# A third GpSimd addition for each group, another table of shared units and slots, and a prologue with two token chains side by side

## The reference

```python
# tokens: b=64, t=128, j=64
h = layernorm(x.reshape(b, t, 192), ln0_g, ln0_b)
h = relu(conv2d(h, conv1_w, conv1_b, ((2, 2), (1, 1))))     # 128 -> 128 channels, 5x3
h = relu(conv2d(layernorm(h), conv2_w, conv2_b, ...))       # 5x2
h = relu(conv2d(layernorm(h), conv3_w, conv3_b, ...))       # 128 -> 256 channels, 5x2
h = layernorm(concat(...)) @ out_w + out_b                  # [b, 128, 64]

# attention on xn = layernorm(h), 8 heads of width 64
v = xn @ wqv_w.T + wqv_b                                    # q, vf, vb
k = xn[:, :, None, :] * wk
a = -sum_w |q[b,s,h,w] - k[b,t,h,w]| / 8                    # L1 distance, no matmul form
a = softmax(concat(a, zeros(1 row)), axis=1)[:, :t]
o = (einsum('bsdh,bshw->bdhw', a, vf) + einsum('bdsh,bshw->bdhw', a, vb)).sum(heads)
h = h + xn + (o * sigmoid(1.702 * o)) @ fanin_w.T + fanin_b

# experts: 32 of width 16, the one with the greatest logit for each token
h = h + relu(relu(xn @ W1[idx] + b1[idx]) @ W2[idx] + b2[idx])   # xn = layernorm(h)
```

## Time and profile before

| | |
|---|---|
| median of three timed executions | 3646.7 us (3644.56 to 3649.15) |
| profiled execution | 3643.14 us, span 3641.3 us |
| mean granted TensorE clock | 0.973 |
| VectorE busy | 3320.0 us (91%), 2699.7 of them direct reductions (2272) |
| TensorE busy | 3261.5 us (90%) |
| ScalarE busy | 2621.0 us (72%), 1863.9 of them absolute values (1824) |
| GpSimd busy | 2435.1 us (67%) |
| accumulating DMAs | 512, 478.18 MB, 66.7% of 16 engines |

### The profile page before, as it was taken

The page is one execution under the profiler, slowest core; times in us unless marked ns, Lnnn a source line. Parts: engine busy times, 40 slices in busy tenths (PEclk is TensorE's granted clock), DMA queues, the critical chain, the costliest instruction groups (busy, mean ns, idle before and its releaser), DMA issues. The chain is left out here.

```text
span 3641.3 us, 77565 instructions
## 1 busy us (share of the span) xinstructions
PE 3261.5 (90%) x23008; PEld 2460.2 (68%) x23008; DVE 3320.0 (91%) x4557; ACT 2621.0 (72%) x4705; POOL 2435.1 (67%) x2212
## 2 busy tenths in 40 slices
PE   5899999999999999999999999999999999999886
PEld 4667667666677666677666677666677666677554
DVE  4899999999999999999999999999999999999885
ACT  1677777777777777777777777777777777777774
POOL 1676667676766766766766676766666766666764
PEclk8999999999999999999999999999999999999998
DMA  1677777777777777777777777777777777777774
GB/s 56 133 156 148 142 144 149 142 150 148 140 145 148 141 157 146 141 144 149 143 151 146 142 142 151 146 147 145 146 142 146 153 145 146 145 144 139 156 143 84
DMA packets 192483, 516.99 MB, mean 142 GB/s; under 512 B 67990, under 2 KB 126230, under 8 KB 151352
## 3 DMA queue, kind: packets, MB, share of 16 engines
q0 software_dynamic: 73728, 478.18, 66.7%
q1 hardware_dynamic: 118712, 38.26, 5.3%
HBM read 10.79 MB, written 2.10 MB: 4 GB/s over the span
## 5 line engine op out<-in xcount | busy, mean ns | idle before, releaser
L788 DVE TENSOR_REDUCE S<-psU 128x16 f32<-128x1024 f32 x2272 | 2699.7, 1215 | 190.2 <-PE psU L387 169.1
L387 PE MATMUL psU<-flat,kT 99*128 99x256 bf16 x16384 | 2304.7, 276 | 233.5 <-DVE S L788 205.2
L587 ACT ACTIVATE absd<-psU 128x1024 f32<-128x1024 f32 x1824 | 1863.9, 1024 | 612.3 <-PE psU L387 589.2
L387 PEld LDWEIGHTS psU<-flat,kT 99*128 99x128 bf16 x16384 | 1508.8, 98 | 871.1 <-DVE S L788 389.3
L1056 POOL TENSOR_TENSOR absd<-absd 128x1024 f32<-128x1024 f32 (+2 forms) x512 | 1111.3, 2171 | 307.5 <-DMA absd<-absd 304.4
L1045 POOL DMA_DIRECT2D absd<-absd x512 | 456.4, 891 | 640.5 <-ACT absd L587 571.0
L1060 POOL TENSOR_TENSOR absd<-absd 128x512 f32<-128x512 f32 (+2 forms) x512 | 586.0, 1145 | 40.1
L400 PE MATMUL psC<-c1in,w 128*128 128x256 f32 (+1 forms) x960 | 347.4, 449 | 21.3 <-DVE c1in L830 21.2
L799 DVE TENSOR_REDUCE S<-absd 128x64 f32<-128x512 f32 (+2 forms) x512 | 315.7, 617 | 7.6 <-POOL absd L1060 7.6
L486 PE MATMUL psZ<-P,v 128*128 128x256 f32 x1024 | 301.3, 387 | 0.8 <-ACT P L701 0.8
L419 PE MATMUL psC<-c3in,w 128*128 128x128 f32 x1280 | 256.2, 286 | 23.1 <-DVE c3in L830 23.1
(11 more groups left out here) (139 smaller groups left out, 2076.1 us busy)
## 6 DMA issues: line engine op xcount, KB each, us to landing
absd<-absd POOLq DMA_DIRECT2D x320, 1024.0 KB, 7.7
absd<-absd POOLq DMA_DIRECT2D x160, 768.0 KB, 6.4
flat<-qparts SPq DMA_DIRECT2D x3072, 8.0 KB, 3.7
absd<-absd POOLq DMA_DIRECT2D x32, 512.0 KB, 4.8
xin<-in_x SPq DMA_DIRECT2D x32, 192.0 KB, 7.0
out_h<-result SPq DMA_DIRECT2D x32, 64.0 KB, 5.7
w<-in_w SPq DMA_DIRECT2D x1, 1280.0 KB
w<-in_w SPq DMA_DIRECT2D x1, 960.0 KB, 5.2
```

The source lines that it names most:

```text
L387: mm = nc.tensor.matmul(psU[:, slot % PLACES, m], kT[0:ROWS + 3, b, m, :], flat[0:ROWS + 3, half % HALVES, :, lo:lo + BLOCK], start=True, ...
L587: nc.scalar.activation(absd[:, c % GROUPS, :, u], psU[:, slot % PLACES].rearrange("p (n a) s w -> p n (a s w)", n=2), ACT.Abs).then_inc(a_ ...
L788: nc.vector.tensor_reduce(S[:, b, hd, SB * c:SB * c + SB], psU[:, slot % PLACES].rearrange("p a s w -> p s a w"), AX.XY, ALU.add, apply_ab ...
```

## The change

1. GpSimd's tree gets a third level. After 16 + 16 and 8 + 8, it now adds 4 + 4, so VectorE's last addition reduces four numbers for each sum and not eight (WIDTH = 4, LEVELS = 3). The tree stands 11 slots behind the group's end and not 10; the last addition stays at 17.
2. 60 of the 128 units are shared and not 57: groups of four, three and two units number 13, 2 and 1, where they numbered 10, 5 and 1.
3. Nearly all slots of the tables move by a few.
4. The prologue has one loop of 256 slots. The chain of pair 0 runs in psL, the second bank of psU's last place, with semaphores of its own (lead_pe and so on), and the chain of pair 1 in psC, 40 slots behind (LEAD). As both share the input tiles c1in, c2in, c3in, resn and resT, the second waits for the first chain's reader in each (`lead(step)`). Norm and keys of pair 0 start at slot 128, the first queries at 128 + QUERY_AFTER = 194 plus their own slots.
5. VectorE's twelve copies into `flat` go. SyncE issues four DMAs with 96 partitions each, as soon as the pattern is there, behind the load of the third pair's input.

```diff
-SHARED = [(0, 2, 4, 6), (0, 2, 4, 6), (1, 3, 5), (0, 2, 4, 6), (0, 2, 4, 6), (0, 2, 4, 6), (1, 3, 5), (0, 2, 4, 6),
-          (0, 2, 4, 6), (0, 2, 4, 6), (0, 4), (2, 4, 6), (0, 2, 4, 6), (0, 2, 4, 6), (0, 3, 6), (0, 2, 4)]
+SHARED = [(0, 2, 4, 6), (0, 2, 4, 6), (0, 2, 4, 6), (0, 2, 4, 6), (1, 3, 5), (0, 2, 4, 6), (0, 2, 4, 6), (0, 2, 4, 6),
+          (0, 2, 4, 6), (0, 2, 4, 6), (0, 2, 4, 6), (3, 6), (0, 2, 4, 6), (0, 2, 4, 6), (0, 3, 6), (0, 2, 4, 6)]
...
-LEVELS = 2
-WIDTH = 32 >> LEVELS
-TREE_AFTER = 10
+LEVELS = 3
+WIDTH = 4
+TREE_AFTER = 11
+LEAD = 40
+QUERY_AFTER = 66
...
-KQ_AT = dict(kT=21, q=13, q_len=1, qpart1=12, qrest1=13, qpart2=28, qpart3=29)
+KQ_AT = dict(kT=21, q=13, q_len=1, qpart1=13, qrest1=14, qpart2=38, qpart3=37)
...
+        psL = psU[:, PLACES - 1, BLOCKS // 2:BLOCKS].rearrange("p m s w -> p (m s w)")
...
             def prologue():
                 load_x(1)
                 load_x(2)
+                sp.wait_ge(pattern_made, 14)
+                for n in range(HALVES):
+                    heads = slice(n % 2 * 4, n % 2 * 4 + 4)
+                    sp.dma_start(flat[0:ROWS, n],
+                                 pattern[0:ROWS, heads].rearrange("p h m w -> p (h m w)").unsqueeze(1)
+                                 .broadcast_to([ROWS, SB, HALF])).then_inc(filled, 16)
...
                 pe.wait_ge(ready, READY)
-                for s in range(SLOTS):
+                for s in range(2 * SLOTS):
                     if s == TOK_AT["conv2"]:
                         pe.wait_ge(loaded, LOADED)
-                    tok(0, s)
-                for s in range(SLOTS):
-                    norm(0, s)
-                    kq(0, 0, s - SECOND)
-                    tok(1, s)
+                    tok(0, s, psL, lead_pe, lead_act, lead_dve)
+                    norm(0, s - SLOTS)
+                    kq(0, 0, s - SLOTS - QUERY_AFTER)
+                    tok(1, s - LEAD)
...
+                def lead(step):
+
+                    if isinstance(p, int) and p == 1:
+                        dve.wait_ge(lead_pe, TOK_PE.after(0, step))
...
                 nc.gpsimd.tensor_tensor(lo, lo, hi, ALU.add).then_inc(a_tree, 1)
+                rows = lo.rearrange("p u (s w) -> p u s w", w=BLOCK)
                 pool.wait_ge(a_tree, LEVELS * (TREES * i + c) + 1)
-                rows = lo.rearrange("p u (s w) -> p u s w", w=BLOCK)
+                lo, hi = rows[:, :, :, 0:8], rows[:, :, :, 8:16]
+                nc.gpsimd.tensor_tensor(lo, lo, hi, ALU.add).then_inc(a_tree, 1)
+                pool.wait_ge(a_tree, LEVELS * (TREES * i + c) + 2)
                 lo, hi = rows[:, :, :, 0:WIDTH], rows[:, :, :, WIDTH:2 * WIDTH]
                 nc.gpsimd.tensor_tensor(lo, lo, hi, ALU.add).then_inc(a_tree, 1)
```

More of the change, by code:

```diff
@@ L362, in unit @@
                 if slot == 0 and isinstance(i, int) and i == 0:
-                    pe.wait_ge(filled, 3 * HALVES)
+                    pe.wait_ge(filled, 16 * HALVES)
+                if slot == PLACES - 1 and isinstance(i, int) and i == 0:
+                    pe.wait_ge(lead_dve, TOK_DVE.after(0, "h"))
                 if slot % 64 == 0:
@@ L395, in tok @@
                     if n == 0:
[L396 to L399 removed]
+                        pe.wait_ge(by_dve, TOK_DVE.after(q, "shifta1"))
+                    o_v = z[:, 0:6 * J].rearrange("p (b j w) -> p b j w", b=2, w=3)
                     mm = nc.tensor.matmul(o_v[:, :, :, o:o + wn], w1[:, 3 * dy + dx, :],
@@ L610, in tok @@
                 if slot == TOK_AT["turn"] + 1:
-                    act.wait_ge(tok_pe, TOK_PE.after(p, "turn"))
-                    nc.scalar.activation(resT[:, :, :], psC[:, 0:2 * T].rearrange("p (b t) -> p b t", b=2),
+                    act.wait_ge(by_pe, TOK_PE.after(q, "turn"))
+                    if isinstance(p, int) and p == 1:
+                        act.wait_ge(lead_pe, TOK_PE.after(0, "out"))
+                    nc.scalar.activation(resT[:, :, :], z[:, 0:2 * T].rearrange("p (b t) -> p b t", b=2),
@@ L835, in after, with tok @@
+            def tok(p, slot, z=psC, by_pe=tok_pe, by_act=tok_act, by_dve=tok_dve, by_pool=tok_pool):
+                q = max(p - 1, 0) if isinstance(p, int) else p - 1
+                def lead(step):
+                    if isinstance(p, int) and p == 1:
+                        dve.wait_ge(lead_pe, TOK_PE.after(0, step))
                 def after(name):
-                    return lambda s: TOK_DVE.after(p, s[:-1] + name + s[-1])
+                    return lambda s: TOK_DVE.after(q, s[:-1] + name + s[-1])
@@ L860, in tok @@
+                    lead("turn")
                     for b in range(2):
                         nc.vector.tensor_scalar(resn[:, b, :], rows(2 * J)[:, b, :], mv["d"][:, b, 0:1],
-                                                rstd["d"][:, b:b + 1], ALU.subtract, ALU.mult).then_inc(tok_dve, 1)
+                                                rstd["d"][:, b:b + 1], ALU.subtract, ALU.mult).then_inc(by_dve, 1)
                 if slot == TOK_AT["out"] + 1:
-                    dve.wait_ge(tok_pe, TOK_PE.after(p, "out"))
+                    dve.wait_ge(by_pe, TOK_PE.after(q, "out"))
@@ L870, in norm @@
             def norm(p, slot):
                 if slot == NORM_AT["stat"]:
-                    dve.wait_ge(tok_dve, TOK_DVE.after(p, "h"))
+                    if isinstance(p, int) and p == 0:
+                        dve.wait_ge(lead_dve, TOK_DVE.after(0, "h"))
+                    else:
+                        dve.wait_ge(tok_dve, TOK_DVE.after(p - 1, "h"))
                     stats(h, "n", norm_dve, lambda s: NORM_DVE.after(p, s))
@@ L998, in prologue @@
                         weigh()
-                        fill(0)
-                    if s == TOK_AT["conv3"]:
-                        fill(1)
-                for s in range(SLOTS):
-                    norm(0, s)
-                    kq(0, 0, s - SECOND)
-                    tok(1, s)
-                    if s == TOK_AT["conv1"]:
-                        fill(2)
+                    norm(0, s - SLOTS)
+                    kq(0, 0, s - SLOTS - QUERY_AFTER)
+                    tok(1, s - LEAD)
             def iteration(i, late=True, tokens=True, ahead=True):
@@ L1124, in prologue @@
                 pool.wait_ge(ready, READY)
-                for s in range(SLOTS):
-                    if s == TOK_AT["conv2"]:
-                        pool.wait_ge(loaded, LOADED)
-                    tok(0, s)
-                for s in range(SLOTS):
-                    norm(0, s)
-                    kq(0, 0, s - SECOND)
-                    tok(1, s)
+                for s in range(2 * SLOTS):
+                    tok(0, s, lead_dve, lead_pool)
+                    norm(0, s - SLOTS)
+                    kq(0, 0, s - SLOTS - QUERY_AFTER)
+                    tok(1, s - LEAD)
             def iteration(i, late=True, tokens=True, ahead=True):
```

155 lines of the change are left out of this document (77 added, 78 removed).

## The result

The changed kernel takes 3586.24 us, the median of three runs (3582.9 to 3590.83), against 3646.7: a ratio of 0.9838, 95% interval 0.9824 to 0.9851. It is faster, by 60 us. I had forecast 3490 us, and 3580 was the upper end of my range: the forecast gain was 157 us, and less than half of it came.

The account below looks back on a forecast made before the run. The bound was taken to alternate in each pair, about 63 us VectorE's and 46 TensorE's. 3643.1 - 144 (loop) - 16 (prologue) + 4.5 (end) = 3487.6, plus 3.6 is 3491, said as 3490 us; 8-in-10 range 3425 to 3580.

Parts of the forecast that it names:

- The prologue: Before the pair loop: overlapped token chains and constant rows filled by DMA start the first unit at 81, not 96.6: -16 us.
- the relief: Pair loop: VectorE loses 7.2 us a pair through fewer reductions and smaller last additions; 4.5 us a pair arrives.
- the term of 144 us: Pair loop: 32 pairs at 4.5 us each, summed stretch by stretch; ends 64 and 230 us.
- rivals C and D: GpSimd's trees: C, they become the bound, 3750 us, chance 0.08; D, their waits eat the loop's gain, 3639 us, 0.05.
- TensorE full: Three stretches of a pair, about 46 us, set by TensorE with no slack, so relief of VectorE gives nothing there.
- VectorE decides: The other four stretches of a pair, about 63 us, set by VectorE, so its relief shows there.
- Rival B: Pair loop: TensorE stays in front in the long stretch too, only the seam gives, 2.0 us a pair: 3571 us, chance 0.20.
- my own stretches: Forecast gains by stretch of a pair; 1.6 us in the 16.80 us stretch and 1.3 in the 6.50 us one.
- Rival A: Pair loop: VectorE's whole cut of 7.2 us a pair arrives, 230 us in all: 3405 us, chance 0.12.
- The end: After the loop: the last group ends later with four units; last issue to last addition takes 12.2 us, +4.5 us in all.

Follow-up runs that it names:

- e1: Only the new prologue, with the slots, 57 shared units and two GpSimd additions of before, against the kernel before: 3617.46 us, 0.9918.
- e4: New prologue and all new slots, with the 57 shared units and two additions of before, against the kernel before: 3717.1 us, 1.0194.
- e3: New prologue, third addition and 60 shared units, with all slots of before, against the kernel before: 3834.58 us, 1.0526.
- e5: Changed kernel with the old table of 57 shared units: 3668.73 us; between its two kinds of pairs, 6.8 us at the half clock cost 2.5 us.
- e6: Changed kernel with each of VectorE's 68 direct reductions a pair reading half its unit (those sums left out): 3596.05 us, 0.9864 of the kernel before.
- e15: Changed kernel without 6 of 15 matmuls of the first convolution and 10 of 20 of the third: 3579.6 us, 0.9813 of the kernel before.
- e13: The new prologue alone (slots, 57 shared units, two additions of before), with each direct reduction reading half its unit: 3452.35 us, 0.9473 of the kernel before.
- e18: New prologue and third addition, slots and 57 shared units of before, but VectorE's last additions 20 slots behind a group, not 17: 3760.58 us, 1.0299.
- e2: New prologue and GpSimd's third addition, with the slots and 57 shared units of before, against the kernel before: 3632.56 us, 0.9961.
- e7: Changed kernel with ScalarE taking absolute values of half of each shared unit (those sums left out): 3553.21 us, 0.9745 of the kernel before.

## Why the prediction was wrong

**The prologue: right.** Forecast -16 us and a first unit at 81. It starts at 82.83, not 96.64, and waits 5.6 us for its rows (I had 3.7, from the earlier trace rows). By itself (e1) the new prologue brought the first unit forward by 16 us; that the kernel gained 23 to 29 is the loop's irregular pairs, which I did not foresee. The row of the changed kernel:

```profile
82.83 6.15 PE L403 MATMUL psU<-flat,kT 99*128 99x256 bf16 x32 [5.64 <-DMA flat<-qparts]
```

**The failed step: the moved slots at nothing, and the relief taken off the old slots' stretches.** The sum went from the earlier trace rows straight to the relief, 4.5 us a pair, and had no term for "Nearly all slots of the tables move". Of the new slots I kept only where units and additions stand. Measured one after the other, the new slots cost 100 us by themselves (e4), and the relief behind them, with the end's few us, gives 131: 3617.5 + 99.6 - 130.9 = 3586.2. Against my terms that is 13 us more from the prologue, 9 less from relief and end together (139.5 forecast), and 100 for the slots: 3491 - 13 + 9 + 100 = 3587.

The split hangs on the order. At the slots that my sum was read from, the relief costs 217 us (e3), and the new slots then give 248: 3617.5 + 217.1 - 248.3 = 3586.2. So the term of 144 us was wrong where it was worked out, in sign too. That 131 lies so near to it at the new slots is luck: at e5's price, an estimate, 58 of the 131 are TensorE's clock coming back (282 us at 1.2 GHz in e4, 122 in the changed kernel), for which the sum had no term.

The diff had candidates for the slots' price in it: the experts' products spread over four slots (14 us), x of the norm behind a root at slot 6 (14 us; both together 22), the convolutions' and the scalings' places. I had the rows of each in the trace of before and worked out none.

**The other work behind the trees.** I asked what GpSimd's other work does to the trees (rivals C and D). The trees came in time in most groups. What did not, at the old slots, was the other work behind them: the experts' root of 1.5 us that ScalarE waits for (10.1 us over the span with two additions, 44.1 with three, 66.0 with 60 units as well), and behind ScalarE the absolute values and TensorE. At the new slots x of that norm stands later and does not wait (3.8 us once, at the end). The seam has a wait of its own instead (27.1 us), but that one came with the slots (23.8 in e4) and not with the third addition.

**"TensorE full" and "VectorE decides" was a reading of busy time, and too sharp.** By it, 33 us less of VectorE should give many us, and 3 to 5 us less of TensorE should show. At the new slots neither gave anything that can be told (e6, e15), and at the old slots VectorE gave 5.2 (e13). In six of the seven stretches of the changed kernel a second engine is within 2 us of the first, and in the long one within 2.8. Rival B had TensorE in front of the long stretch; that stretch did stay, and B's 3571 us is nearest to the result, but its mechanism is not what e15 shows, and its number is luck: it took 2.0 us a pair for the seam, where my own stretches have 1.6 + 1.3 = 2.9, which gives 3542. (D's sum gives 3635 us, not 3639.) Rival A and the rule beside it fall: the page Perfetto Trace Analysis of the Trainium skill (Identifying the Most-Contended Engine) would go by TensorE's weight loads, 74.73 of 107.30 (and by the share of its peak arithmetic, which no view here shows), and so make VectorE the one bound; e6 took a third of VectorE's work away and the time stayed. At the new slots neither busy time named the bound.

**The end: right.** From the last issue at 3535.11 to the last addition at 3546.58 it is 11.5 us, forecast 12.2, where it was 8.7:

```profile
3535.11 0.87 POOL L1061 DMA_DIRECT2D absd<-absd  x1
```
```profile
3546.58 0.42 DVE L816 TENSOR_REDUCE S<-absd 128x64 f32<-128x256 f32 x1 [6.66 <-POOL absd L1079]
```

**Left open.** Which of the moved slots makes up the rest of the 100 us; why TensorE's clock falls in slots 0 to 15 of e18, and so why it is slower than e2 when a wait of VectorE goes; and what the floor of 106 us a pair at the new slots is, since no engine's work alone sets it.

## What to carry to other kernels

When a change moves a whole table of slots, price the table by itself, and price the rest of the change on both tables: here the same relief gave 131 us on the new one and cost 217 on the old, so neither term could be added to the other as it stood. When an in-order engine gets a longer instruction sequence, list what stands behind the sequence on its queue and who waits for each of those, not only who waits for the sequence. An engine that is full in a stretch is a bound only for as much as it stands above the next: take work off by test, or take the difference of the two busy times as a first estimate of what a relief can give. In the earlier trace rows VectorE's differences to the next engine add up to 5.6 us a pair (2.6, 1.0, 0.2 and 1.8), and e13 gave 5.2. It is no upper limit: ScalarE is the busiest engine in no stretch of the changed kernel, and its relief gave 1.6 (e7).
